# Attention block 2 of a Perceiver layer: the value product in column groups, probabilities transposed into the staging buffer, the last exponentials with a bias, another order for V, and one weight split held back

## The reference

```python
q, k, v = (proj(Wq), proj(Wk), proj(Wv))            # of layernorm(x)
a_q, a_k, a_v = Eq[rel], Ek[rel], Ev[rel]
logits = (einsum('bhld,bhmd->bhlm', q, k) + einsum('bhld,lmd->bhlm', q, a_k)
          + einsum('bhmd,lmd->bhlm', k, a_q) + einsum('lmd,lmd->lm', a_q, a_k)) * scale
attn = softmax(logits, axis=-1)
out = einsum('bhlm,bhmd->bhld', attn, v) + einsum('bhlm,lmd->bhld', attn, a_v)
x = x + out.transpose(0, 2, 1, 3).reshape(B, S, D)
```

## Time and profile before

| | |
|---|---|
| median of 3 runs | 875.81 us (875.32 to 876.31) |
| the profiled execution: its own time | 876.13 us |
| its span in the trace | 874.3 us |
| PE busy | 802.9 us (92%) |
| VectorE, ScalarE, GpSimd busy | 632.2, 474.8, 469.7 us |
| share of the chain that ended last | PE 81%, VectorE 10%, ScalarE 6% |

### The profile page before, as it was taken

How to read it: one execution, slowest core, us unless ns; L and a number is a source line. 1 busy time by engine, 2 the same in 40 slices (tenths; PEclk the granted TensorE clock), 3 DMA queues, 4 the chain that set the end, 5 groups by cost and what they waited for, 6 DMA issues and landing times.

```text
span 874.3 us, 14940 instructions
## 1 busy us (share of the span) xinstructions
PE 802.9 (92%) x6354; PEld 603.7 (69%) x6354; DVE 632.2 (72%) x511; ACT 474.8 (54%) x645; POOL 469.7 (54%) x253
## 2 busy tenths in 40 slices
PE   4998899999999999999999999999389978959788
PEld 2576677777777777777777777777266767957677
DVE  5126988889878888788887888879863289065685
ACT  4356674764756747557475574754533445203382
POOL 0033778688677685776867768676831102222200
PEclk9999999999999999999999999999688989568899
DMA  7100101101101011010110101100114996020101
GB/s 282 51 13 36 49 1 49 49 2 49 34 16 49 2 49 47 3 49 1 49 49 1 50 1 49 49 1 2 48 50 174 378 373 249 1 85 1 49 1 49
DMA packets 15330, 55.57 MB, mean 64 GB/s; under 512 B 1696, under 2 KB 2080, under 8 KB 11680
## 3 DMA queue, kind: packets, MB, share of 16 engines
q1 hardware_dynamic: 15264, 54.61, 17.3%
HBM read 43.13 MB, written 11.47 MB: 62 GB/s over the span
## 4 chain that ended last, share of the span: by engine, by line
PE 81%; DVE 10%; ACT 6%; issue 3%; POOL 0%; ACTq 0%; DVEq 0%; POOLq 0%
PE ps L344 23%; PE ps L327 22%; PE ps L391 13%; PE ps L409 7%; PE ps L559 3%; PE ps L354 3%; PE ps L335 2%; PE ps L421 2%; ACT s_buf L749 1%; PE ps L480 1%; ACT v_buf L732 1%; DVE blocks L1211 1%; PE ps L569 1%; ACT s_buf L740 1%; DVE rmax L1225 1%
## 5 line engine op out<-in xcount | busy, mean ns | idle before, releaser
L988 POOL TENSOR_TENSOR s_buf<-s_buf,r_all 128x1024 f32<-128x1024 f32 x93 | 196.6, 2150 | 11.2 <-DVE r_all L1144 11.2
L740 ACT COPY s_buf<-ps 128x1024 f32<-128x1024 f32 x128 | 129.7, 1013 | 60.6 <-PE ps L391 60.6
L391 PE MATMUL ps<-q_blk,k_t 64*128 64x256 f32 x1024 | 145.2, 402 | 5.8 <-ACT s_buf L740 5.8
L1102 DVE TENSOR_REDUCE extra<-s_buf 128x128 f32<-128x2048 f32 x48 | 109.4, 2280 | 41.7 <-ACT s_buf L740 41.7
L749 ACT ACTIVATE s_buf<-s_buf 128x1024 f32<-128x1024 f32 x128 | 135.4, 1063 | 0.0
L391 PEld LDWEIGHTS ps<-q_blk,k_t 64*128 64x128 f32 x1024 | 88.1, 186 | 52.9 <-issue 39.2
L724 ACT ACTIVATE k_t<-ps,cols 128x512 f32<-128x512 f32 x64 | 44.0, 688 | 128.2 <-PE ps L327 128.2
L1124 DVE TENSOR_TENSOR s_buf<-s_buf,ps 128x2048 f32<-128x2048 f32 x48 | 106.9, 2283 | 0.5
L1131 DVE TENSOR_REDUCE ps<-s_buf 128x128 f32<-128x4096 f32 x16 | 70.8, 4428 | 48.8 <-ACT s_buf L749 48.8
L966 POOL TENSOR_TENSOR odd_lo<-raw,odd_hi 128x512 fp32r<-128x512 f32 x32 | 41.4, 1293 | 113.5 <-ACT odd_hi L717 113.5
L971 POOL TENSOR_TENSOR w_lo<-raw,w_hi 128x2048 fp32r<-128x2048 f32 x8 | 36.4, 4547 | 120.4 <-ACT w_hi L709 120.4
(11 more groups left out here) (185 smaller groups left out, 1400.3 us busy)
## 6 DMA issues: line engine op xcount, KB each, us to landing
raw<-in_ctxT SPq DMA_DIRECT2D x16, 1024.0 KB, 4.9
rel_scratch<-blocks SPq DMA_DIRECT2D x16, 636.0 KB, 10.7
s_buf<-rel_scratch SPq DMA_DIRECT2D x7, 1210.0 KB, 9.7
raw<-in_Wk SPq DMA_DIRECT2D x2, 1024.0 KB, 4.7
raw<-in_Wq SPq DMA_DIRECT2D x2, 1024.0 KB, 7.2
raw<-in_Wv SPq DMA_DIRECT2D x2, 1024.0 KB, 5.8
extra<-in_EvRel SPq DMA_DIRECT2D x1, 2048.0 KB, 12.6
extra<-rel_scratch SPq DMA_DIRECT2D x1, 1210.0 KB, 10.0
```

The costliest lines, as they stand in the source:

```text
L391: last = mm(ps[:, 2 + half_rows, i * 2 * P:(i + 1) * 2 * P], k_t[rows, hg, b * P:(b + 1) * P], q_blk[rows, b * C + hg, :], start=True, sto ...
L740: copy(piece(t, p).rearrange("p e (u n) -> p (e u) n", u=2), ps[:, 2:4, :]).then_inc(s["s_evac"], 1)
L988: pool.tensor_tensor(part, part, spread(r_all, 4), ALU.mult).then_inc(s["attn_pool"], 1)
L1102: nc.vector.tensor_reduce(m_ps if k == 0 else m_next[:, k % 2, :], over_pairs(t, 2 * k, 2), AX.XY, ALU.max).then_inc(s["max_done"], 1)
```

## The change

Six edits go together:

1. The value product of stage 2 is written as that of stage 3: V's 32 columns are stationary, the probabilities move (128 columns), and the heads of a group go to four bands of PSUM partitions. Its result is transposed (dimension by row), so ScalarE copies it to `k_t`, and a new `attended_t(b)` on PE transposes it back after the first bank of the Ev product; VectorE scales it in place in PSUM.
2. The transposed probabilities go to `probs_t(u)` in `blocks` instead of over `lg_all`. `at_copy(u)` no longer waits for the sum; the first one waits for the scratch stores that read this buffer. The Ev product reads them from there.
3. For the last group VectorE does not subtract the maximum; it scales 128x16 maxima by `-SCALE`, and ScalarE takes 16 exponentials of 128x128 with that as a bias, one head each. The transposes of this group start by batch.
4. The copies of group 2 go to VectorE, and its sums are moved behind them.
5. V of batch 1 is projected ahead of the transposes of group 0, into a bank of its own, and the waits of the later ones are finer.
6. In stage 3 GpSimd's `weight_lo(6)` waits for the 128x64 product (`q3_rsp`).

The diff, without the list of semaphore names and two renamed calls of `probs3` in stage 3:

```diff
@@ -184,7 +184,7 @@
         def lg3(u):
             return s_buf[:, 0, u * H:(u + 1) * H, :]
 
-        def probs3(u):
+        def probs_t(u):
             return blocks[:, u * B:(u + 1) * B]
 
         names = """x_in wq_in wk_in wv_in cols_in bv_in bo_in tab_in ctx_in ctx_hi ctx_lo wkv_hi wkv_lo wraw_in wsplit_hi wsplit_lo
...
@@ -484,11 +484,10 @@
             def values2(b, bank):
                 if b == 0:
                     weight_ready(3)
+                if b < 2:
                     pe.wait_ge(s["rk_evac"], 2 * C)
-                elif b == 1:
-                    pe.wait_ge(s["at_done"], B)
                 else:
-                    pe.wait_ge(s["at_done"], 2 * B)
+                    pe.wait_ge(s["at_done"], B + b - 1)
                 proj_n(1, bank, s["v2_psum"], b)
 
             def logits(u):
...
@@ -511,14 +510,18 @@
 
             def attention_t(u):
                 base = 0 if u < 2 else 4
-                pe.wait_ge(s["exp2"], u + 1)
-                if u < 2:
-                    pe.wait_ge(s["v2_evac"], u + 1)
-                else:
+                if u < C - 1:
+                    pe.wait_ge(s["exp2"], u + 1)
+                if u == 0:
+                    pe.wait_ge(s["v2_evac"], 2)
+                elif u == 2:
                     pe.wait_ge(s["lg_done"], C)
-                if u in (1, 3):
-                    pe.wait_ge(s["at_done"], B * u)
                 for b in range(B):
+                    if u == 1:
+                        pe.wait_ge(s["at_done"], b + 1)
+                    if u == C - 1:
+                        pe.wait_ge(s["at_dve"], b + 1)
+                        pe.wait_ge(s["exp2"], C + b)
                     for j in range(J):
                         last = nc.tensor.transpose(ps[:, base + b, j * P:(j + 1) * P], lg_all[:, u, b, j, :], ident[:])
                     last.then_inc(s["at_psum"], 1)
...
@@ -541,9 +544,9 @@
             logits(1)
             values2(0, 0)
             logits(2)
+            values2(1, 1)
             attention_t(0)
             logits(3)
-            values2(1, 0)
             attention_t(1)
             attention_t(2)
             values2(2, 0)
...
@@ -552,22 +555,36 @@
 
             pe.wait_ge(s["v2_evac"], B)
             for hg in range(C):
-                pe.wait_ge(s["at_done"], B * (hg + 1))
+                if hg < 2:
+                    pe.wait_ge(s["at_done"], B * (hg + 1))
+                elif hg == 2:
+                    pe.wait_ge(s["at_dve"], B)
                 for b in range(B):
+                    if hg == C - 1:
+                        pe.wait_ge(s["at_done"], 2 * B + b + 1)
                     for j in range(J):
                         part = slice((hg * J + j) * HD, (hg * J + j + 1) * HD)
-                        last = mm(ps[:, b, part], lg_all[:, hg, b, j, :], v_buf[:, 1, b, part], start=True, stop=True,
-                                  skip_group_check=True)
+                        last = mm(ps[j * HD:(j + 1) * HD, b, hg * P:(hg + 1) * P], v_buf[:, 1, b, part],
+                                  probs_t(hg)[:, b, j, :], start=hg == 0, stop=hg == C - 1, skip_group_check=True)
                     if hg == C - 1:
                         last.then_inc(s["av2"], 1)
 
+            def attended_t(b):
+                pe.wait_ge(s["av2_evac"], b + 1)
+                for hg in range(C):
+                    last = nc.tensor.transpose(ps[:, b, hg * P:(hg + 1) * P], k_t[:, b, hg * P:(hg + 1) * P], ident[:])
+                last.then_inc(s["av2_t"], 1)
+
             pe.wait_ge(s["ev_in"], 16)
             for bank in range(4):
+                if bank == 1:
+                    for b in range(B):
+                        attended_t(b)
                 for n in range(8):
                     for i in range(4):
                         l = i * HD + bank * 8 + n
                         last = mm(ps[i * HD:(i + 1) * HD, 4 + bank, n * 64:(n + 1) * 64], ev_rel[:, l, :],
-                                  lg_all[:, :, :, :, l].rearrange("p u b j -> p b u j"), start=n == 0, stop=n == 7,
+                                  blocks[:, :, :, l].rearrange("p (u b) j -> p b u j", u=C), start=n == 0, stop=n == 7,
                                   skip_group_check=True)
                 last.then_inc(s["ev2"], 1)
 
...
@@ -843,14 +860,23 @@
 
             def exp2(u):
                 act.wait_ge(s["sub2"], u + 1)
-                nc.scalar.activation(lg(u), lg(u), ACT.Exp, scale=SCALE).then_inc(s["exp2"], 1)
+                if u < C - 1:
+                    nc.scalar.activation(lg(u), lg(u), ACT.Exp, scale=SCALE).then_inc(s["exp2"], 1)
+                    return
+                for b in range(B):
+                    for n in range(b * J, b * J + J):
+                        last = nc.scalar.activation(lg(u)[:, n, :], lg(u)[:, n, :], ACT.Exp, scale=SCALE,
+                                                    bias=rmax[:, u * H + n:u * H + n + 1])
+                    last.then_inc(s["exp2"], 1)
 
             def at_copy(u):
-                act.wait_ge(s["sum2"], u + 1)
                 base = 0 if u < 2 else 4
+                if u == 0:
+                    for n in range(SLOTS):
+                        act.wait_ge(s[f"rel_out_{n}"], 16 * len(range(n, NROUND, SLOTS)))
                 for b in range(B):
                     act.wait_ge(s["at_psum"], B * u + b + 1)
-                    copy(lg_all[:, u, b], ps[:, base + b, :].rearrange("p (j l) -> p j l", j=J)).then_inc(s["at_done"], 1)
+                    copy(probs_t(u)[:, b], ps[:, base + b, :].rearrange("p (j l) -> p j l", j=J)).then_inc(s["at_done"], 1)
 
             keys2(0)
             queries2(0)
...
@@ -865,16 +891,18 @@
             exp2(0)
             values2(0, 0)
             exp2(1)
+            values2(1, 1)
             at_copy(0)
             exp2(2)
             weight_hi(4)
-            values2(1, 0)
             at_copy(1)
             exp2(3)
-            at_copy(2)
             values2(2, 0)
             values2(3, 1)
             at_copy(3)
+            for b in range(B):
+                act.wait_ge(s["av2"], b + 1)
+                copy(k_t[:, b, :], ps[:, b, :]).then_inc(s["av2_evac"], 1)
             weight_hi(5)
             for b in range(B):
                 ln_std(2, b)
...
@@ -1020,6 +1048,7 @@
             pool.wait_ge(s["b3_in"], 16)
             bp = bias3[:, 2:3, :].broadcast_to([P, B, D])
             pool.tensor_tensor(x_res[:], x_res[:], bp, ALU.add).then_inc(s["xp_done"], 1)
+            pool.wait_ge(s["q3_rsp"], 1)
             weight_lo(6)
             weight_lo(7)
 
...
@@ -1224,10 +1253,14 @@
                 dve.wait_ge(s["lg_done"], u + 1)
                 nc.vector.tensor_reduce(rmax[:, u * H:(u + 1) * H], lg(u), AX.X, ALU.max).then_inc(s["max2"], 1)
                 dve.wait_ge(s["max2"], u + 1)
-                tt(lg(u), lg(u), keys(rmax, u), ALU.subtract).then_inc(s["sub2"], 1)
+                if u < C - 1:
+                    tt(lg(u), lg(u), keys(rmax, u), ALU.subtract).then_inc(s["sub2"], 1)
+                    return
+                top = rmax[:, u * H:(u + 1) * H]
+                nc.vector.tensor_scalar(top, top, -SCALE, None, ALU.mult).then_inc(s["sub2"], 1)
 
             def total2(u):
-                dve.wait_ge(s["exp2"], u + 1)
+                dve.wait_ge(s["exp2"], u + 1 if u < C - 1 else C - 1 + B)
                 nc.vector.tensor_reduce(rsum[:, u * H:(u + 1) * H], lg(u), AX.X, ALU.add).then_inc(s["sum2"], 1)
 
             for hg in range(C):
...
@@ -1237,23 +1270,26 @@
             softmax2(0)
             add2(1)
             softmax2(1)
-            total2(0)
             add2(2)
             softmax2(2)
-            total2(1)
+            total2(0)
             add2(3)
             softmax2(3)
-            total2(2)
-            total2(3)
+            for b in range(B):
+                dve.wait_ge(s["at_psum"], 2 * B + b + 1)
+                nc.vector.tensor_copy(probs_t(2)[:, b],
+                                      ps[:, 4 + b, :].rearrange("p (j l) -> p j l", j=J)).then_inc(s["at_dve"], 1)
+            for u in range(1, C):
+                total2(u)
             dve.wait_ge(s["sum2"], C)
             nc.vector.reciprocal(rinv[:], rsum[:]).then_inc(s["rinv2"], 1)
 
             dve.wait_ge(s["rinv2"], 1)
             for b in range(B):
-                dve.wait_ge(s["av2"], b + 1)
-                tt(by_head(v_buf[:, 0, b, :]), by_head(ps[:, b, :]), per_head(rinv, b), ALU.mult).then_inc(s["av2_mul"], 1)
+                dve.wait_ge(s["av2_t"], b + 1)
+                tt(by_head(ps[:, b, :]), by_head(ps[:, b, :]), per_head(rinv, b), ALU.mult).then_inc(s["av2_mul"], 1)
                 dve.wait_ge(s["av2_mul"], b + 1)
-                tt(x_res[:, b, :], x_res[:, b, :], v_buf[:, 0, b, :], ALU.add).then_inc(s["av2_done"], 1)
+                tt(x_res[:, b, :], ps[:, b, :], x_res[:, b, :], ALU.add).then_inc(s["av2_done"], 1)
 
             def ev_transpose(b):
                 if b == 0:
```

## The result

| | before | changed |
|---|---|---|
| median | 875.57 us (4 runs, 874.47 to 876.31) | 850.21 us (4 runs, 845.79 to 851.69) |
| ratio | | 0.9703, 95% interval 0.9666 to 0.974 |
| profiled execution, its span | 876.13, 874.3 us | 849.88, 848.1 us |

What follows compares the result with a forecast made beforehand. PE was busy 92%, but the prediction followed the chain of waits on the edited stretches, including value product 24.00 us and Ev product 7.85 us. 876.13 - 20.8 - 5.5 = 849.8, median 0.3 lower: 849.5 us; range 846.5 to 855.0.

Steps and rivals of the forecast that it cites:

- The value product: Stage 2 on PE: 128 records at 30.6 ns, the price of the same form in stage 3, 3.9 us against 24.0.
- the serial bands: Rival in the value product: bands run one after the other, 121 ns a record, 15.5 us, total 861.1 us; chance 0.04.
- The small wait: Sign named for the value product: a small wait before its last quarter; no size given.
- The Ev product: Stage 2 on PE: 7.85 us carried over, with 0 added for the moving operand's step of 512 bytes instead of 636.
- The bound of 7.85 us: Upper bound on what the new 512-byte step could add to the Ev product: twice the time, +7.85 us.
- I am wrong if Ev's records grow: Sign against the forecast in the Ev product, which was expected at 31 ns a record.
- the slow rival: Rival in the Ev product: the 512-byte step makes columns queue for one piece of memory; 140 ns a record, 877.2 us; chance 0.02.
- The transposes back: 16 transposes on PE between bank 0 and bank 1 of the Ev product: 1.94 us at full clock, high end 1.7 more.
- The start of the value product: Stage 2, worked forward from VectorE's rows: start at 741.0, a gain of 2.7 us.
- The scale: Scaling of group 3's maxima on VectorE: 0.2 us if free, but waits for GpSimd's split to 735.4; not-held rival 848.0 us, chance 0.12.
- The exponentials: 16 on ScalarE for the last group: 0.29 us from start to start, 4.7 us in all, to 740.1.
- The held-back split: Stage 3: 128x64 product 3.95 to 0.2 us, query transposes 1.73 us shorter, 5.5 us in all; rival of less gain, chance 0.13.

Runs made afterwards that it cites:

- the old form in new surroundings: Changed kernel with the value product back in its old form, no transposes back, no copy to `k_t`: 870.40 us, ratio 0.9952.
- the seven traces: Kept traces with the same instructions up to the value product: changed kernel, its second run, five experiments (stage 3 split, old form, three steps); product starts 45.41 to 46.46 us behind logits.
- two batches: The unedited changed kernel measured twice: 850.21 us (4 runs), and 848.75 us (5 runs) as yardstick beside two versions that go further.

## Why the prediction was right, step by step

- **The value product, 3.9 us predicted, 3.70 measured.** Taking the price from the rows of the same form in stage 3 held, and the serial bands (15.5 us) are out. What the prediction did not need, and the old form in new surroundings showed, is that nearly half of its 24 us was the clock. The small wait that was forecast before the last quarter did not come: the product has no gap.
- **The Ev product, the one mis-sized term.** I took 0 for the new step because old and new both jump between elements. It cost +1.62 us, and four other steps show that it is 512 itself. The bound of 7.85 us was wide enough, and the value that I chose at its low end was wrong. "I am wrong if Ev's records grow" was one of the signs named, and they did grow, from 30.7 to 37.0 ns: on this term the prediction failed by its own sign, though the total came out. Whether it is the queue of the slow rival, at 37 ns a record and not 134, no run shows; that rival's 140 ns a record would also give 877.5 us, not 877.2.
- **The transposes back, 1.94 predicted, 1.90 measured,** and VectorE's scale and add stayed covered (over at 752.81, 2.9 us ahead of the Ev product), as forecast.
- **The start of the value product, -2.7 predicted, -2.21 measured.** The scale was held by GpSimd's split, as I let it be (3.73 us, until 734.84). Most of the 0.5 us is the split itself: I let it begin where it did before, but its weight's load released it, and by the common count it began 0.4 us later. Over the seven traces it began 34.96 to 36.00 us behind the logits, against 35.61 before, and the mean start of the product, 46.03, is what was forecast (741.0 - 695.04 = 45.96). The exponentials came 0.29 us apart (4.79 us for 16, of 0.39 each), as I took them to; but the two rows that I read this from, 829.10 and 829.41, are 0.31 apart, so that term was nearer than its source.
- **What I gave edits without testing them.** Undone one by one, the order of V is worth 2.2 to 2.6 us, as much as the whole earlier start, and the bias form 0.3 us. The prediction summed them in one timeline and did not say so. The transposed probabilities in `blocks` and the copies of group 2 on VectorE (edits 2 and 4) were never undone; what they give is not shown.
- **The held-back split, 5.5 predicted, 5.3 by undoing it.** Both halves came: 3.70 us of wait and 1.7 us of clock (1.61 where it was undone). The other 0.7 us of the -6.10 lies behind the layernorm of stage 3, where the first 12 matmuls took 4.09 us instead of 4.81. It is no effect of the change: the changed kernel's second run has 4.40 there, and the experiments 3.58 to 4.99, as the clock comes back sooner or later.

The sum was right in part by luck: the +1.62 of the Ev product was offset by 0.7 us behind the layernorm and 0.85 us ahead of the logits of group 0 that belong to no edit. The medians of this kernel's two batches, 850.21 and 848.75 us, are further apart than the forecast and the first of them.

## What to carry to other kernels

When a changed product exists elsewhere in the same trace, take its whole price from there, loads included. When a moving or strided operand gets a new step, don't carry its price over at nothing, least of all if the step becomes 512 bytes: pad the row by a few elements and look, as one element was enough here. And before an operation on VectorE is made small to shorten the path, see what GpSimd is doing then: here a 16-column operation waited 3.7 us, and moving GpSimd's work gave about 2 us, the rewriting 0.3. And run the same kernel twice before a piece of half a microsecond is explained.

## What the hardware showed that was not expected

- A step of 512 bytes between the moving elements costs 37.0 ns a record, steps of 516, 528, 532 and 636 bytes 29.6 to 31.0.
- PE's clock fell to 1.2 GHz within the old value product, with PE busy all the time since the product began, in both traces that have it, and stayed there for over 20 us at 100% busy. In the new form it stays at 2.4 GHz; but that one is over after 3.70 us, and in the old one the fall came at 742.5 us after a start at 740.01, and at 747.1 after a start at 743.71. Whether a longer product of the new form would keep the clock is not shown.
- A VectorE operation of 128x16, SBUF to SBUF, waited for the end of GpSimd's operation just as one of 128x2048 did in the earlier trace rows: 3.72 us against 0.17. The small one ended 0.03 us behind GpSimd's split, the large one 2.15 us (737.35 against 735.20), nearly its whole length of 2.3.
